# A fused vision-text layer on one core: stage order by list scheduling, loads as stages, bf16 splits on GpSimd

## The reference

```
h = concat(patches @ W.T + b (36, a class row ahead) + pos, txt)   # 4 x 549 x 192
q, k, v = heads(layernorm(h) @ w_qkv + b_qkv)
mem     = heads(memory @ w_mem + b_mem)
o = softmax(q k.T / 4) v + softmax(q mem.T / 4) mem
h = h + o @ w_out + b_out
x = layernorm(h)
p = softmax(x @ router_w.T);  two largest -> experts, weights
h = h + sum over the two of weight * (gelu(x @ w1[e]) @ w2[e])
```

## Time and profile before

| | us |
|---|---|
| median of 3 runs | 731.89 (727.23 to 737.56) |
| profiled execution | 729.53 |
| its span | 727.6 |
| TensorE busy | 589.1 |
| VectorE busy | 451.3 |
| ScalarE busy | 354.6 |
| GpSimd busy | 167.1 |

### The profile page before, as it was taken

One profiled execution on the slowest core, in us unless ns is written; L12 is line 12 of the kernel. 1 busy time (PEld: TensorE's weight loads), 2 busy tenths in 40 slices (PEclk: granted clock), 3 DMA queues, 4 the chain that ended last, 5 costly groups with the idle time before them and its releaser, 6 DMA issues.

```text
span 727.6 us, 14692 instructions
## 1 busy us (share of the span) xinstructions
PE 589.1 (81%) x5165; PEld 435.8 (60%) x5166; DVE 451.3 (62%) x1026; ACT 354.6 (49%) x664; POOL 167.1 (23%) x144
## 2 busy tenths in 40 slices
PE   3886989789889899899899976300489999999993
PEld 1541455456555555466466654300489999999992
DVE  2458665577668767688578526489546565656561
ACT  3420356466746655655656883422034444444441
POOL 3000000000000000000002334555136565566542
PEclk9975599899989989999899998555589999999997
DMA  7057002510038010061121135431013333333322
GB/s 227 1 142 92 1 1 83 125 32 2 3 119 117 1 56 1 4 189 47 49 95 46 45 91 138 140 125 50 14 35 50 50 55 53 56 50 50 51 43 23
DMA packets 35164, 46.49 MB, mean 64 GB/s; under 512 B 7860, under 2 KB 29861, under 8 KB 35114
## 3 DMA queue, kind: packets, MB, share of 16 engines
q1 hardware_dynamic: 26720, 35.10, 19.2%
q0 software_dynamic: 8064, 9.64, 8.1%
q10 hardware_dynamic: 330, 1.07, 0.4%
HBM read 31.26 MB, written 14.19 MB: 62 GB/s over the span
## 4 chain that ended last, share of the span: by engine, by line
PE 56%; DVE 18%; DMA 8%; SPq 6%; ACT 5%; issue 5%; POOL 1%; DVEq 0%; ACTq 0%; POOLq 0%
PE rings L695 11%; PE psS L695 9%; PE psO L917 9%; PE psO L820 6%; PE rings L776 6%; PE psS L805 5%; DVE mx L1052 5%; SPq L430 5%; PE rings L903 3%; DMA out<-yb,row 3%; DMA stage<-in_w 2%; DMA parts_transposed<-partsT 2%; PE psO L826 1%; DVE mt L1054 1%; POOL w1b L493 1%
## 5 line engine op out<-in xcount | busy, mean ns | idle before, releaser
L618 ACT ACTIVATE pr<-psS 128x732 f32<-128x732 f32 x180 | 138.4, 780 | 87.0 <-PE psS L805 66.7
L1052 DVE TENSOR_REDUCE mx<-rings 128x1 f32<-128x512 f32 x192 | 126.7, 685 | 70.3 <-PE rings L776 67.6
L776 PE MATMUL rings<-kst,qst 96*128 96x512 bf16 (+1 forms) x480 | 109.2, 329 | 16.8 <-DMA kst<-parts_transposed 7.1
L496 POOL TENSOR_TENSOR w1a_low<-stage,w1a_high 128x512 fp32r<-128x512 f32 x12 | 14.9, 1269 | 408.7 <-ACT w1a_high L652 408.7
L805 PE MATMUL psS<-qst,kst 100*128 100x183 bf16 x720 | 90.6, 251 | 10.5 <-ACT pr L618 7.5
L805 PEld LDWEIGHTS psS<-qst,kst 100*128 100x128 bf16 x720 | 61.5, 101 | 35.0 <-ACT pr L618 10.5
L523 POOL DMA_INDIRECT out<-yb,row x42 | 66.4, 1582 | 69.4 <-ACT yb L671 56.2
L917 PE MATMUL psO<-w,hTh 128*128 x252 | 80.9, 370 | 1.3 <-DVE hTl L1218 1.3
L820 PE MATMUL psO<-pr,val 128*32 128x183 f32 x1440 | 75.6, 339 | 0.0
L665 ACT ACTIVATE hTh<-rings 128x384 fp32r<-128x384 f32 x84 | 36.7, 489 | 76.0 <-PE rings L903 76.0
L776 PEld LDWEIGHTS rings<-kst,qst 96*128 96x128 bf16 (+1 forms) x480 | 35.1, 102 | 61.2 <-DVE mx L1052 21.5
(11 more groups left out here) (170 smaller groups left out, 1116.8 us busy)
## 6 DMA issues: line engine op xcount, KB each, us to landing
stage<-in_w SPq DMA_DIRECT2D x10, 768.0 KB, 4.2
parts_transposed<-partsT SPq DMA_DIRECT2D x4, 1440.0 KB, 5.1
kst<-parts_transposed SPq DMA_DIRECT2D x72, 80.0 KB, 3.3
qst<-parts_transposed SPq DMA_DIRECT2D x72, 68.6 KB, 3.0
stage<-in_w SPq DMA_DIRECT2D x8, 384.0 KB, 5.7
rows<-in_txt SPq DMA_DIRECT2D x4, 384.0 KB, 7.3
out<-rows SPq DMA_DIRECT2D x16, 96.0 KB
normalised<-rows SPq DMA_DIRECT2D x16, 96.0 KB
```

The costliest lines, as they stand in the source:

```text
L618: act.activation(pr[:, n % PB], psS[:, n % 2, :, 0:2 * QC], ACT.Exp, scale=HD ** -0.5).then_inc(s_exp, 1)
L776: ins = pe.matmul(bank(s + (0,))[r:r + n, c:c + k1 - k0], qst[sl][0:KQ, h, t * P:t * P + n], kst[sl][0:KQ, h, k0:k1], start=True, stop=True)
L1052: ins = dve.tensor_reduce(mx[0:n, g % 2, t, j:j + 1], bank(s + (0,))[0:n, :], AX, ALU.max)
```

## The change

LEAD becomes 16, the bursts go, and `plan()` puts its stages into seven streams, each with due times: scores, values with keeps, images, maxima, the rest (fronts, merges, gates), loads, weights. A class `Clocks` models the engines with a fixed cost for each kind of stage and remembers when each result is there (`needs()` lists what a stage waits for). The list is then made step by step: of the heads of the streams, as far as they are due within AHEAD units, that stage is taken for which TensorE would be idle the shortest, plus PULL for each unit by which it is ahead of the most overdue, plus MODE where it changes between values and other products. `front(0)`, the images, the maxima of group 0 and the first weight chunks go through the same choice; what stands behind the attention keeps its order.

The loads of a group become a stage of their own, `load`, with SyncE's wait for the store in it. `split` of tiles 5 to 19 is done by GpSimd, with a semaphore of its own (`s_split_pool`), which the copies of `qk`, the transposes of `stack` and the weight copies wait for; batch 0 stays on VectorE.

The order written out by the new `plan()` has these differences in place: `swap` of batches 1 to 3 stands behind scores 9, 54 and 100 (before 14, 59 and 104); the first maxima of the next batch behind 22, 67 and 112, as before; the 180 values and their keeps come in 99 bursts (before 72); `wload` 4 and 5 stand behind score 168 (before 178 and 179); ahead of the first score stand 17 maxima of group 1 (before 13) and the front of tiles 5 and 6 up to the first `stack`.

```diff
-LEAD = 8
+LEAD = 16
...
+LAG = 0.21
+MODE = 0.11
+SPAN = {"img": 2.3, "xT": 0.25, "qk": 1.46, "v": 0.74, "maxT": 0.46, "norm": 0.34, "attT": 0.25, "proj": 0.70, "ln2T": 0.25,
+        "router": 0.34, "score": 0.325}
+PULL = 0.1
+AHEAD = 24.0
+
...
+    if kind == "score":
+        return (([("exp", i - 2)] if i >= 2 else []) + ([("value", i - PB)] if i >= PB else []) +
+                ([("offset", i // (NC * TT))] if i % (NC * TT) == 0 else []))
+    if kind == "value":
+        return [("exp", i)] + ([("keep", i // TT - 1)] if i % TT == 0 and i else [])
+    if kind == "keep":
+        b = i // (G * NC)
+        return [("value", i * TT + TT - 1)] + ([("att", (b - 1) * TT - 1)] if b >= 2 else [])
...
+    def idle(self, s):
+        when, i = self.ready(s), s[1]
+        if when is None:
+            return None
+        if span(s) is None:
+            engine = "POOL" if s[0] == "split" and i >= TT else {"keep": "ACT", "whi": "ACT", "swap": "SP", "load": "SP", "wload": "SP"}.get(s[0], "DVE")
+            return max(0.0, when - max(self.now[engine], self.now["PE"]))
+        if s[0] not in ("score", "value"):
+            when = max(when, self.free[self.jobs % R])
+        return max(0.0, when - self.now["PE"]) + (MODE if (s[0] == "value") != self.columns else 0.0)
+    def issue(self, s):
+        kind, i, at, on = s[0], s[1], self.at, self.on
+        when, end, done = self.ready(s), None, None
+        if span(s) is not None:
+            ring = kind not in ("score", "value")
+            if ring:
+                slot = self.jobs % R
+                self.jobs += 1
+                when = max(when, self.free[slot])
+            end = on("PE", span(s) + (MODE if (kind == "value") != self.columns else 0.0), when) + LAG
+            self.columns = kind == "value"
+            at[s] = end
...
+        elif kind == "split":
+            at[s] = (on("DVE", 0.95, when) if i < TT else on("POOL", 1.8, when)) + 0.08
...
+        elif kind == "swap":
+            at[s] = on("SP", 0.4, when)
+            at[("swapped", i)] = at[s] + 5.0
+        elif kind == "load":
+            at[s] = on("SP", 5.5, when)
+            at[("loaded", i * G + s[2])] = at[s] + 2.3
...
+        elif kind == "rstd":
+            at[s] = on("DVE", 0.9, on("ACT", 3.2, on("DVE", 0.25)))
...
-    burst = lambda c, k0, k1: [("value", c * TT + k) for k in range(k0, k1)] + ([("keep", c)] if k1 == TT else [])
-
     units, NG = TT * NC, B * G
-    fill = []
-
-    def spread(stages, start, end):
+    scores, values, images, maxes, rest, loads, weights = streams = [[] for _ in range(7)]
+    def spread(stream, stages, start, end):
 
         cost = [WORK.get(s[0], 0.1) for s in stages]
         done = 0.0
         for s, c in zip(stages, cost):
-            fill.append((start + (end - start) * (done + c / 2) / sum(cost), len(fill), s))
+            stream.append((start + (end - start) * (done + c / 2) / sum(cost), s))
             done += c
 
+    for n in range(NG * units):
+        k = n % TT
+        scores.append((n - 1.0, ("score", n)))
+        values.append((n - k + (2.0 if k < 2 else 5.0), ("value", n)))
+        if k == TT - 1:
+            values.append((n + 1.0, ("keep", n // TT)))
+    spread(rest, front(0), -40.0, -20.0)
+    loads += [(-20.0 + j, ("load", 0, j)) for j in range(G)]
+    spread(images, [s for b in range(1, B) for s in [("img", b)] + [("moments", b * TT + t) for t in range(TT)]] +
+           [("first", 1)], -20.0, -12.0)
+    spread(maxes, maxima(0) + [("maxT", 0)], -12.0, -1.0)
     for g in range(1, NG):
-
-        spread(maxima(g), units * (g - 2 + PHASE), units * (g - 1 + PHASE))
-        fill.append((units * (g - 1 + PHASE) + 3.5, len(fill), ("maxT", g)))
+        spread(maxes, maxima(g), units * (g - 2 + PHASE), units * (g - 1 + PHASE))
+        maxes.append((units * (g - 1 + PHASE) + 1.5, ("maxT", g)))
+    maxes.sort(key=lambda z: z[0])
     for b in range(B):
         at = b * G * units
         if b + 1 < B:
-            spread(front(b + 1), at, at + units * (1 + PHASE) - LEAD)
+            spread(rest, front(b + 1), at, at + units * (1 + PHASE) - LEAD)
+            loads += [(at + units * (1 + PHASE) - LEAD + 3.0 * j, ("load", b + 1, j)) for j in range(G)]
         if b > 0:
-            spread(merge(b - 1) + gate(b - 1), at + (units * (1 + PHASE) - LEAD if b + 1 < B else 0), at + G * units)
+            spread(rest, merge(b - 1) + gate(b - 1), at + (units * (1 + PHASE) - LEAD if b + 1 < B else 0), at + G * units)
...
-    spread(early, (NG - G) * units + 1, NG * units)
-    fill.sort()
-
-    order = front(0) + [s for b in range(1, B) for s in [("img", b)] + [("moments", b * TT + t) for t in range(TT)]]
-    order += [("first", 1)] + maxima(0)
-    order += [("maxT", 0)]
-    for n in range(NG * units):
-        if n == 0:
-            order += [s for x, _, s in fill if x < 0]
-            order.append(("score", 0))
-        if n + 1 < NG * units:
-            order.append(("score", n + 1))
-        if n % TT == 0 and n > 0:
-            order += burst(n // TT - 1, 2, TT)
-        if n % TT == 2:
-            order += burst(n // TT, 0, 2)
-        order += [s for x, _, s in fill if n <= x < n + 1]
-    order += burst(NG * NC - 1, 2, TT)
+    spread(weights, early, (NG - G) * units + 1, NG * units)
+    order, clocks, head = [], Clocks(), [0] * len(streams)
+    while any(h < len(x) for h, x in zip(head, streams)):
+        first = [(x[h][0], n, x[h][1]) for n, (h, x) in enumerate(zip(head, streams)) if h < len(x)]
+        due = min(x for x, _, _ in first)
+        choice = [(clocks.idle(s) + PULL * (x - due), x, n, s) for x, n, s in first
+                  if x <= due + AHEAD and clocks.idle(s) is not None]
+        _, _, n, s = min(choice)
+        clocks.issue(s)
+        order.append(s)
+        head[n] += 1
...
+        def split_done(eng, i, step):
+            eng.wait_ge(*((s_split, 2 * i + step + 1) if i < TT else (s_split_pool, 2 * (i - TT) + step + 1)))
...
+                elif s[0] == "load":
+                    _, b, j = s
                     sp.wait_ge(s_swap, 16 * (b + 1))
                     if b >= 2:
                         sp.wait_ge(s_score, (b - 1) * G * NC * TT)
-                    for j in range(G):
-                        if b >= 1:
-                            sp.wait_ge(s_load[j], 16 * 2 * 6 * b)
-                        for dst, row0, cols, which in ((qst, 0, T, Q_PARTS), (kst, D, KEYS, K_PARTS)):
-                            heads = slice(j * GH, (j + 1) * GH)
-                            src = swap[b, row0:row0 + D].rearrange("(h d) s t -> d h s t", d=HD)
-                            for k, part in enumerate(which):
-                                sp.dma_start(dst[b % 2][k * HD:(k + 1) * HD, heads, :],
-                                             src[:, heads, part, 0:cols]).then_inc(s_load[j], 16)
+                    if b >= 1:
+                        sp.wait_ge(s_load[j], 16 * 2 * 6 * b)
+                    for dst, row0, cols, which in ((qst, 0, T, Q_PARTS), (kst, D, KEYS, K_PARTS)):
+                        heads = slice(j * GH, (j + 1) * GH)
+                        src = swap[b, row0:row0 + D].rearrange("(h d) s t -> d h s t", d=HD)
+                        for k, part in enumerate(which):
+                            sp.dma_start(dst[b % 2][k * HD:(k + 1) * HD, heads, :],
+                                         src[:, heads, part, 0:cols]).then_inc(s_load[j], 16)
...
+            steps = [0]
+            def link(ins):
+                steps[0] += 1
+                ins.then_inc(s_pchain, 1)
+                pool.wait_ge(s_pchain, steps[0])
+            split_done(pool, TT - 1, 1)
             for s in ORDER:
-                if s[0] == "whi":
+                if s[0] == "split" and s[1] >= TT:
+                    _, i, step = s
+                    n = rows_of(i % TT)
+                    high, middle, low = (qkp[0:n, i % 2, part, :] for part in range(3))
+                    if step == 0:
+                        drained(pool, ("qk", i, 0))
+                        job_done(pool, ("stack", i - 2, 1, 0))
+                        link(pool.tensor_copy(high, qk[0:n, i % 2, :]))
+                        link(pool.tensor_tensor(rest[0:n, :], qk[0:n, i % 2, :], high, ALU.subtract))
+                    else:
+                        link(pool.tensor_copy(middle, rest[0:n, :]))
+                        link(pool.tensor_tensor(low, rest[0:n, :], middle, ALU.subtract))
+                    pool.sem_inc(s_split_pool, 1)
+                elif s[0] == "whi":
...
-                        act.wait_ge(s_split, 2 * (i - 2) + 1)
+                        split_done(act, i - 2, 0)
...
-                        act.wait_ge(s_split, 2 * NT)
+                        split_done(act, NT - 1, 1)
...
-                    pe.wait_ge(s_split, 2 * i + 2)
+                    split_done(pe, i, 1)
...
                 elif kind == "split":
+                    if i >= TT:
```

(55 more changed lines are left out.)

63 lines of the change are left out of this document (added).

## The result

| | before | after |
|---|---|---|
| median, us | 731.2 (727.23 to 737.56) | 700.63 (699.98 to 702.36) |
| profiled execution, us | 729.53 | 700.95 |
| its span, us | 727.6 | 698.7 |

The account below looks back on a forecast made before the run. TensorE, busy 81%, was taken as the limit, with a 60 us pot of idle time and lower clock in the attention. Gains of 32.4 less costs of 5.3, 2 and 4 gave -21 on 729.5: 708 us, range 690 to 733.

Parts of the forecast that it names:

- Loads: Batch 1's loads and score 30's offsets: earlier swap takes back 9 of 12.1 us lost, some 2 us of wait stay.
- Fronts: Projections of the next batch: transposes no longer wait for splits queued between VectorE's maxima; 6 of 9.1 us idle taken back.
- Behind the fronts: Stretch from 208.7, after batch 2's front: half the clock's loss, 1.4 us, and 1 of 1.95 idle taken back.
- Gates: Two gate stretches: table loads stay, more TensorE work covers them; idle and half the clock's loss, 7 us with shorter ring waits.
- Weights: Behind the attention: wload 4 and 5 land earlier, ScalarE's 4.03 us wait goes and the last merge moves up; -4 us.
- the lock: Rival, fronts: GpSimd and VectorE share a lock, slowing normalisations that fall into splits; 717 us, chance 0.05.
- Head: First stretch: more maxima and part of a front done before score 0; 4 (0 to 7) of 9.4 us taken back.
- mode switches: Cost on TensorE: 27 more bursts of values at 0.2 us each, 5.3 us.
- the delay on GpSimd: Cost in three fronts: a tile's split takes at most 4.3 us, covered by 4.8; +2 us for the last tiles.
- the waits only move: Rival: clock falls as often, gate and front waits keep their size, only loads, tail and half a front won; 720 us, 0.23.
- GpSimd paces the fronts: Rival: a split slower than 4.8 us a tile stops TensorE fifteen times; 738 us at 6.8 a tile, chance 0.12.
- The whole pot: Rival: all waits and clock falls go except ScalarE's at the end and score 30's; 678, more likely 685 us; chance 0.10.

Follow-up runs that it names:

- e5: Changed kernel with the loads of groups 1 and 2 of batches 1 to 3 moved behind the next maxT: 693.62 us.
- e9: Kernel before with LEAD 16 for 8 and each later batch's swap moved behind the maxT it would block: 715.45 us.
- e7: Kernel before with the layer norms' Ln replaced by Copy, so ScalarE loads no tables there: 723.67 us.
- e6: Changed kernel with the layer norms' Ln replaced by Copy, so ScalarE loads no tables there: 690.92 us.
- e12: e5 with the planner's MODE at 0.38 instead of 0.11, giving 72 bursts of values instead of 99: 691.29 us.
- e8: Kernel before with its values in 141 bursts instead of 72, all else in place: 757.39 us.
- e1: Changed kernel with every split back on VectorE, new order kept: 707.66 us.
- e2: Changed kernel with the plan() of before (LEAD 8, loads directly behind swap), splits still on GpSimd: 727.58 us.
- e11: e5 with the last layer norm moved ahead of two weight copies: 688.68 us.
- e4: Changed kernel with weight loads 4 and 5 put back in their old places: 698.81 us.

## Why the prediction was right, and where its sum was off

The forecast was 708 us, the time 700.6: the mechanism held, and the sum was 7 short. The profiled span fell by 28.9 where 21 were forecast. Term by term, from the table (prediction, measured):

- Loads, -9: -4.2 over scores 15 to 45. The waits came out as worked out: 0.80 at the first maxima, and 2.50 at score 30, where I had left some 2 standing. What I took back too readily is the rest: 3.9 us stay idle in scores 15 to 30, and the clock behind score 30 is 0.84, some 2.9 us, for which I had counted nothing. The order had it to give: e5 gets 9.1.
- Fronts, -6: -3.4 in the second and third. Idle time fell by more than forecast, from 4.8 in each to 0.9, but the third runs at a clock of 0.92 and gives some 3 back.
- Behind the fronts, -2.4: -6.1. I halved the idle time and the clock's loss behind the front of batch 2, where both went whole (4.4), and left out the front of batch 3 (1.7). e9 has as much in the old order, 6.4.
- Gates, -7: -9.8. The size was near, the reason wrong in part. I wrote that their idle time is one event, the table loads. e7 takes these away in the old order, where 3.3 and 3.2 us stay idle; e6 takes them away in the new one, where 0.4 and 0.5 do. Other waits stood beside the table loads; the new order removed most of them, and the table loads, worth 4.2 and 2.5 there (e6), are what remains. The second gate's clock is 1.00 with them (0.89 before); e9 has that gate at 27.2 and 1.00 in the old order.
- Weights, -4: -2.3 between the last score and the end. The 3.9 was won at the table load, and 1.7 of the refinement's 3.3 us are new (it took 1.6 before): the lock that I had as a rival for the fronts took its price at the tail.
- Head, -4: -5.1.
- From score 135 to the last: 0 forecast, +2.0 measured.

These come to -28.9 with whatever the costs took; mine came to -32.4 before 11.3 of costs. The terms miss by 1 to 5 us both ways, so that their sum came near is in part luck. The step that failed is the costs. The 5.3 for mode switches does not show: 27 fewer bursts give 2.3, within the interval, and nothing in the twelve stretches (e12). That fits a planner that weighs the wait and chooses small bursts where they are free; a fixed order that takes them everywhere pays up to 0.38 each, longer waits and a lower clock included (e8). The 2 for the delay on GpSimd does not show either: of TensorE's listed waits between 60 and 410 us one names GpSimd, 0.3 us ahead of a transpose of parts. The tile's 4.0 is 3.16, the casts half of my nearest row. The 4 for a fixed order's waits has no place of its own; what is left of such waits is score 30's.

The experiments also divide the gain otherwise than I did. Fronts and split together were -6 +2 = -4, as the relief of VectorE was booked with the fronts; the splits on GpSimd are worth 4 to 7 (e1, e2), and in the new order they are all that shortens the fronts (e1). The other terms and costs come to -17.1; the new order without GpSimd gives 24 (e1). VectorE was not the bound on the mean, 62 to 69% busy in the fronts, but it was what TensorE's longest waits in the old fronts name.

Of the rivals, "the waits only move" falls with the fronts and gates. "GpSimd paces the fronts" needed casts of 2.1 and they take 0.50. The whole pot was not reached by this kernel, but e11 comes within 4 us of its 685. The lock in the fronts is small: the normalisations of a full tile take 400 ns on the mean for 373 before.

Two of the Trainium skill's rules were weighed. GPSIMD Engine Reference, "Engine selection", would leave elementwise work on VectorE. The prices agree in their direction: a subtraction takes 0.92 against VectorE's 0.56, and the cast, which the page puts near VectorE's rate, 0.50 against 0.35 (e1). The advice does not hold for this kernel: the slower engine was free. SBUF — State Buffer, "SBUF: two separate sides", gives the lock to whichever instruction starts first, for its whole length. The 1.19 beside GpSimd's subtractions (7.50 for six, 1.25 each) agrees, and so does e11's 0.17.

What stays open: why the third front's clock was 0.92 in the changed kernel and 1.00 with the loads apart (it is 0.92 in e1, e4 and e6 too, in e6 behind a gate at 1.00, and 1.00 in e11); and how much of the first front's 5.9 in e9 is the clock's and how much the waits'.

## What to carry to other kernels

A queue that issues transfers in order is part of the schedule: before moving a block of loads, list what stands behind it there and when that is due. Here the same constant costs 27 us with the swap ahead of the offsets' stage and gains 16 with it behind. And an engine that is far from being the bound on the mean can still be the next in line inside one stage, so work taken from it there has a value; ask stage by stage, by taking the suspected wait away alone, before crediting it with the idle time beside it.

## What the runs showed of the hardware

- VectorE operations of 128x5 took 0.77 to 1.19 us beside GpSimd's subtractions and 0.17 without, in the same kernel and across kernels. The three slow ones of the changed kernel end at 430.78, 432.00 and 433.23, and three of GpSimd's subtractions, an estimate from equal sixths of the 7.50, at 430.71, 431.96 and 433.21.
- A cast of 128x384 to bf16 took 0.50 us on GpSimd and 0.35 on VectorE; a tile of 37 rows costs GpSimd the same 0.50.
- Removing a wait of 2.5 us for offsets brought the granted clock of the following 16 us from 0.84 to 1.00: the clock's share (2.2 us) was nearly as large as the wait's own (e5). In e6, with the loads in their place, that wait was 1.2 us and the clock behind it 1.00 as well:

```profile
138.50:154.00 15.50, 15.37 (x214) 9.54 (x215) 10.07 (x20) 12.17 (x19) 0.00 (x0) 1.00 0.01 3
```
